# Cross-attention and block-scaled FFN on one core: GpSimd's second inverse root ahead of a partition maximum, with four lists rearranged around it

## The reference

```
query, key = ctx @ Wq.T + bq, ctx @ Wk.T + bk
attention  = softmax(query @ key.T)                    # (4, 512, 512)
x = x + layernorm(x) @ attention.T                     # stage 1
n = layernorm(x)
h = silu(mx(n) @ mx(gate_w).T) * (mx(n) @ mx(up_w).T)
x = x + mx(h) @ mx(down_w).T                           # stage 2
```

## Time and profile before

| what | value |
|---|---|
| median of 3 runs | 619.66 us (618.08 to 621.9) |
| time of the profiled execution | 622.69 us |
| its span, first to last instruction | 620.9 us |
| PE busy | 599.4 us, 97% of the span |
| DVE busy | 517.3 us, 83% |
| ACT busy | 266.3 us, 43% |
| POOL busy | 43.3 us, 7% |

### The profile page before, as it was taken

The page is one execution under the profiler, slowest core; times in us unless marked ns, Lnnn a source line. Parts: engine busy times, 40 slices in busy tenths (PEclk is TensorE's granted clock), DMA queues, the critical chain, the costliest instruction groups (busy, mean ns, idle before and its releaser), DMA issues.

```text
span 620.9 us, 7042 instructions
## 1 busy us (share of the span) xinstructions
PE 599.4 (97%) x2572; PEld 270.7 (44%) x2572; DVE 517.3 (83%) x518; ACT 266.3 (43%) x341; POOL 43.3 (7%) x49
## 2 busy tenths in 40 slices
PE   8798788999999999999999999999999999999997
PEld 3244344444444444444444444444444444444443
DVE  4999789989999989889889996888199369978931
ACT  3789678274443545542424323422132133424310
POOL 0011120210000000200000000000000001000100
PEclk9999799999999999999999999999999999999999
DMA  8949989579688676655503008400440276257670
GB/s 330 367 98 211 268 264 220 126 195 222 160 164 242 138 203 144 145 103 115 122 2 69 0 1 153 85 1 0 86 84 2 28 142 128 59 119 136 118 136 35
DMA packets 146289, 81.00 MB, mean 130 GB/s; under 512 B 134096, under 2 KB 134096, under 8 KB 142672
## 3 DMA queue, kind: packets, MB, share of 16 engines
q1 hardware_dynamic: 142512, 64.30, 43.2%
q0 software_dynamic: 3744, 16.25, 12.4%
HBM read 26.02 MB, written 8.39 MB: 55 GB/s over the span
## 4 chain that ended last, share of the span: by engine, by line
PE 76%; DVE 8%; issue 7%; DMA 4%; ACT 3%; POOL 1%; DVEq 0%; ACTq 0%; POOLq 0%
PE G L703 46%; PE A L718 27%; DMA W<-hT 3%; PE A L681 2%; DMA gu_hi<-hT 1%; DVE W L1416 1%; PE G L643 1%; DVE W L1309 1%; DVE h L1297 1%; DVE scale L1403 1%; ACT hT L884 1%; PE G L668 1%; PE A L660 1%; DVE h L1292 1%; POOL gu_lo L546 0%
## 5 line engine op out<-in xcount | busy, mean ns | idle before, releaser
L703 PE MATMUL G<-gu_hi,xT 128*128 128x512 f16 x1024 | 306.2, 379 | 0.5 <-DVE h L1457 0.5
L703 PE MATMUL G<-gu_lo,xT 128*128 128x512 f16 x512 | 194.0, 379 | 0.0
L718 PE MATMUL A<-dn,hT 128*128 128x512 f16 x768 | 167.1, 379 | 0.0
L703 PEld LDWEIGHTS G<-gu_hi,xT 128*128 128x128 f16 x1024 | 100.2, 98 | 121.9 <-issue 1.4
L718 PEld LDWEIGHTS A<-dn,hT 128*128 128x128 f16 x768 | 75.1, 98 | 90.6
L978 ACT ACTIVATE silu<-G,unscale 128x512 f32<-128x512 f32 x64 | 43.8, 685 | 146.9 <-PE G L703 121.8
L703 PEld LDWEIGHTS G<-gu_lo,xT 128*128 128x128 f16 x512 | 50.1, 98 | 60.7 <-issue 0.7
L681 PE MATMUL A<-dn,h 128*128 128x512 f32 x128 | 59.3, 619 | 8.6 <-DVE dn L1341 3.7
L1457 DVE SCALAR_TENSOR_TENSOR h<-G,unscale,silu 128x512 f32<-128x512 f32 x64 | 46.6, 736 | 14.7 <-PE G L703 13.3
L1511 DVE SCALAR_TENSOR_TENSOR W<-h,W 128x2048 f16<-128x2048 f32 x15 | 34.3, 2285 | 22.4 <-DMA hT<-W 17.8
L1292 DVE SCALAR_TENSOR_TENSOR h<-mag,h 128x2048 f32<-128x2048 bf16 x18 | 41.1, 2283 | 9.8 <-ACT mag L871 9.7
(11 more groups left out here) (92 smaller groups left out, 465.2 us busy)
## 6 DMA issues: line engine op xcount, KB each, us to landing
W<-in_units SPq DMA_DIRECT2D x12, 1024.0 KB, 5.9
W<-hT POOLq DMA_DIRECT2D x11, 1024.0 KB, 6.0
h<-in_xcols SPq DMA_DIRECT2D x4, 1024.0 KB, 12.9
out_y<-y POOLq DMA_DIRECT2D x14, 256.0 KB, 5.1
h<-in_xrows SPq DMA_DIRECT2D x3, 1024.0 KB, 12.1
out_y<-h SPq DMA_DIRECT2D x3, 1024.0 KB, 8.8
gu_hi<-in_ctxT SPq DMA_DIRECT2D x4, 512.0 KB, 10.6
W<-out_y SPq DMA_DIRECT2D x2, 1024.0 KB, 6.0
```

The costliest lines, as they stand in the source:

```text
L703: last = pe.matmul(dst[:, :], xT[:, b % 2, part, k, :], w[:, c, g, j * 512:(j + 1) * 512], start=(m == 0), stop=(m == 3 * HT - 1))
L718: last = pe.matmul(bank[:, :], hT[:, r % 2, a, k, :], dn[:, w, k, :], start=(m == 0), stop=(m == 3 * IT - 1))
```

## The change

Only the order of calls changes; no instruction is added or dropped, apart from GpSimd's exchanges of code, which are placed by the order of its calls. On SP the low part of unit 1 is transposed before three plain transfers instead of after them. On GpSimd `first_norm(1)` goes in front of `units_max(1)`. On ScalarE `take_probs(0, 0)` and both `take_projection(2, ...)` go forward, `row_variances(1)` goes forward, and `unit_hi(2)` goes behind the row sums of batch 2 and the magnitude of unit 3. On VectorE `units_power(1)` and `unit_dequant(2)` go behind the divide of unit 3, the row statistics of batch 0, its variance and one `add_attended`.

```diff
--- before.py
+++ after.py
@@ -429,10 +429,10 @@
             load_unit(3)
             after_rest("u1")
             turn_unit_hi(1)
+            turn_unit_lo(1)
             load_columns(2)
             store_rows(0)
             load_unit(4)
-            turn_unit_lo(1)
             turn_unit_hi(2)
             after_rest("u2")
             load_rows(3)
@@ -587,8 +587,8 @@
             unit_rest(0)
             after_turn("u0", 1)
             unit_rest(1)
+            first_norm(1)
             units_max(1)
-            first_norm(1)
             second_norm(0)
             after_turn("u2", 0)
             unit_rest(2)
@@ -1023,19 +1023,19 @@
             take_projection(1, 1)
             unit_magnitude(0)
             divide(0, 0)
+            take_probs(0, 0)
             exponential(1, 0)
+            take_projection(2, 0)
             row_sums(1, 0)
             row_sums(1, 1)
-            take_probs(0, 0)
+            take_projection(2, 1)
             row_sums(1, 2)
             row_sums(1, 3)
             divide(0, 1)
             row_means(1)
             exponential(1, 1)
             divide(0, 2)
-            take_projection(2, 0)
             divide(0, 3)
-            take_projection(2, 1)
             unit_magnitude(1)
             unit_hi(0)
             take_projection(3, 0)
@@ -1060,6 +1060,7 @@
             exponential(2, 3)
             row_squares(1, 2)
             row_squares(1, 3)
+            row_variances(1)
             divide(2, 0)
             take_probs(1, 0)
             take_probs(1, 1)
@@ -1067,15 +1068,14 @@
             take_probs(1, 2)
             take_probs(1, 3)
             divide(2, 1)
-            row_variances(1)
             divide(2, 2)
             divide(2, 3)
-            unit_hi(2)
             row_sums(2, 0)
             row_sums(2, 1)
             row_sums(2, 2)
             row_sums(2, 3)
             unit_magnitude(3)
+            unit_hi(2)
             row_means(2)
             exponential(3, 0)
             exponential(3, 1)
@@ -1567,15 +1567,15 @@
             add_attended(0, 3)
             unit_scale(3)
             unit_pull(2)
-            units_power(1)
             row_stats(0, 0)
-            unit_dequant(2)
             unit_divide(3)
             row_stats(0, 1)
             row_stats(0, 2)
             row_stats(0, 3)
             add_attended(1, 0)
             rows_variance(0)
+            units_power(1)
+            unit_dequant(2)
             add_attended(1, 1)
             row_max(3, 0)
             row_max(3, 1)
```

## The result

| | before | after |
|---|---|---|
| median of 12 runs each, side by side on one chip | 618.48 us (617.08 to 622.77) | 622.74 us (621.48 to 623.88) |
| time of the profiled execution | 622.69 us | 621.48 us |
| its span | 620.9 us | 619.7 us |

The changed kernel is slower: 1.0041 times the time before, 95% interval 1.0021 to 1.0061 (worked out from the rounds, so not the quotient of the two medians). Forecast was a gain of 1.4. Between the two profiled executions there is a gain of 1.2, and between the medians a loss of 4.3. The profiled execution before was among the longest of its kernel (622.77 is the only longer one of the twelve), the one after is the shortest of its twelve. So the profile after is read in two steps: was the walk of the changed kernel right, and what was it compared with.

What follows compares the result with a forecast made beforehand. TensorE's unbroken stream from the first product sets the end. Of 6.5 us, 2.2 survives the exchanges, 2.1 goes to slow clock, and earlier VectorE/ScalarE work leaves 1.4: 619.66 - 1.4 = 618.3 us, range 614.9 to 622.3.

Steps and rivals of the forecast that it cites:

- the forecast beside the median is 619.66 - 1.4: Whole kernel: the profiled execution's predicted saving of 1.4 taken off the median of the runs, giving 618.3 us.
- 6.5 us on the table: TensorE's batch 1 attends: removing a 3.74 hole and 2.77 of slow clock would end them at 76.0, not 82.5.
- `first_norm(1)` near 57.3, batch 1 in one piece to 76: GpSimd runs `first_norm(1)` before the maximum; TensorE's four batch 1 attends then run without the 3.74 hole.
- Exchange toward the maximum 6.02, away from it 9.3: GpSimd's code exchanges around the maximum: 6.02 before, 9.3 after (ends 8.4 and 10.3), with the maximum itself 2.22.
- `take_probs(2, 0)` at 80.8, attends of batch 2 at 84.2, clock falls, 2.1 charged: ScalarE gains 2.2 ahead of batch 2; TensorE's hole of some 3.5 brings the clock down, costing 2.1.
- ScalarE's early edits and the fall near 33 us hidden: Early `take_probs(0, 0)` and `take_projection(2, ...)` priced at nothing; a clock fall near 33 us hidden behind VectorE's pace.
- SP's move priced at nothing: SP's reordered transposes and loads: `unit_rest(2)` at about 77.2 against 76.8, batch 3's rows load near 82.75, no cost.
- The spread of the runs, 618.08 to 621.9, taken as noise: Earlier runs' spread: about 1% (6.2 us) is what can be told from no change; within 1% given 0.88.
- A: GpSimd's exchanges cost 6.0 both ways, `second_norm(0)` at 72.6; gain allowed 4.4, time 615.3; chance 0.16.
- B: TensorE's clock holds ahead of batch 2, the 2.1 not paid; gain 2.2 to 2.8, 616.9 to 617.5; chance 0.16.
- C: Both GpSimd exchanges take 10.26, `second_norm(0)` at 81.1; 3.7 slower, 623.4; chance 0.13.
- D: Kernel's end: the gain returns as a longer TensorE wait on VectorE's hidden product; 619.7; chance 0.12.

Runs made afterwards that it cites:

- long course: Executions of the kernel before as first profiled: maximum 2.22, exchange behind it 10.26, `first_norm(1)` at 70.66, first product at 115.64; profiled execution 622.69 us.
- short course: Executions of the unchanged kernel before with maximum 0.38, exchange behind it 8.44, `first_norm(1)` at 67.55, first product at 111.19; profiled execution 617.6 us.
- after_again: The changed kernel, unchanged, run again beside the kernel before: 623.48 us against 617.94, ratio 1.0072.
- after_noroot: The changed kernel with all inverse roots taken off GpSimd, VectorE multiplying by a constant instead: 620.43 us, ratio 1.0003.
- before_noroot: The kernel before with all inverse roots taken off GpSimd, VectorE multiplying by a constant instead: 617.69 us, ratio 0.9957.
- after_fill2: The changed kernel with 21 idle matmuls between the transposes of batch 2's probabilities, 76 to 84 us: 621.16 us, ratio 1.0000.
- after_act_back: The changed kernel with `take_probs(0, 0)` and both `take_projection(2, ...)` back in their old places on ScalarE: 623.49 us, ratio 1.0071.
- after_fill12: The changed kernel with 21 idle matmuls at 76 to 84 us and 16 more in TensorE's hole at 31.5 to 35 us: 621.74 us, ratio 1.0015.
- after_sp_back: The changed kernel with only SP's order put back, unit 1's low part behind the three plain transfers: 622.91 us, ratio 1.0052.
- after_pool_back: The changed kernel with GpSimd's old order, maximum ahead of `first_norm(1)`: 620.51 us, ratio 1.0028.
- after_loads_late: The changed kernel with the three plain transfers issued behind unit 2's high part on SP: 626.68 us, ratio 1.0104.
- before_again: The kernel before, unchanged, run again for its spread: 620.86 us (617.14 to 623.11), ratio 0.9994.
- before_fill46: The kernel before with 12 idle matmuls in TensorE's hole between batch 0's second and third attend, 46.3 to 49.3 us: 622.02 us, ratio 1.0026.
- both_front: A separate version with both inverse roots ahead of the maximum, unit 2's chain and SP's transfers moved to match: 629.77 us, ratio 1.0160.
- before_sp: The kernel before with only SP's move, unit 1's low part transposed ahead of the three plain transfers: 620.99 us, ratio 1.0035.

## Why the prediction was wrong

**The step that failed** is the last one of the sum: "the forecast beside the median is 619.66 - 1.4", 618.3, where 622.74 was measured. It took the profiled execution for an ordinary one that happens to be 3.03 long throughout, so that a saving found in it could be taken off the median. But the 3.03 were not spread over the kernel. They came with the very hole and slow clock that the change removes: the first product is 4.45 later in the long profile than in the short one. The "6.5 us on the table" lie there in the long course alone. An execution of the short course has none of it, and can only pay what the change pushes back.

That step is 3.03 of the 4.4 by which the forecast was missed. The other 1.4 is the walk itself: it gave 621.3 for the changed kernel, and the median is 622.74. The term that was too small there is the exchange away from the maximum with the power and the product behind it, 9.3 + 1.3 = 10.6: 11.72 in the profile of the shortest execution (74.39 + 2.44 less 65.11), 13.13 in after_again, the longest. In the first of these the maximum, 1.85 shorter than charged, made good for it. That the walk meets this profile to 0.3 at the product is in part luck.

**What it pays** can be read between the two profiles of the short course and of the changed kernel. `second_norm(0)` starts at 74.39 against 70.09, 4.3 later. `take_probs(2, 0)` starts at 80.40 against 77.30. The attends of batch 2 begin at 84.17 against 80.63, 3.5 later, and take 2.2 longer at the slow clock. Against that the changed kernel reaches batch 3 with less in the way (3.74 from the last attend of batch 2 to the first of batch 3, 4.99 in the short course), and has no idle 1.06 in front of the product. At the product 3.3 are left (114.48 against 111.19); in after_again it is 6.0 (117.16). The medians are 4.3 and 5.5 apart. By parts, in the group of after_again: 3.0 is the swap on GpSimd and 2.6 the other moves, by the ratios 2.7 and 1.7. The firmest figure for the other moves is after_noroot less before_noroot, 2.7, since neither of these kernels is split as the kernel before is. ScalarE's early moves are none of it.

Point by point, the steps of the prediction:

- *What bounds the kernel, and that the end follows the first product:* held in every profile, 504.6 to 505.8 us between the two.
- *`first_norm(1)` near 57.3, batch 1 in one piece to 76:* held (57.48, 75.86).
- *Exchange toward the maximum 6.02, away from it 9.3:* held in the first profile (6.21, 9.28). Over the others the second ranged from 9.28 to 10.57 with this order of transfers, so 9.3 was at the short end. The maximum's 2.22 was not paid, 0.37; the power and the product behind it were longer than 1.3 instead (2.44 to 76.83 in the first profile, 2.85 in after_again).
- *`take_probs(2, 0)` at 80.8, attends of batch 2 at 84.2, clock falls, 2.1 charged:* held in the first profile (80.40, 84.17, 0.50 from 82 to 88, 2.2), and after_fill2 shows that it is the clock. *End of batch 2 at 100.3, batch 3 at 103.9, product at 114.2:* held there (100.37, 104.11, 114.48), in the shortest execution; in after_again the same three are 103.03, 106.78 and 117.16.
- *ScalarE's early edits and the fall near 33 us hidden:* held, after_act_back and after_fill12.
- *SP's move priced at nothing:* half wrong. `unit_rest(2)` came at 77.29 as forecast and the load of batch 3's rows at 83.27, so against the long course it is nearly free. Against the short course it and the moves that came with it cost some 2 to 3 (1.7 to 3.0 by the pairs above). In that course `unit_rest(2)` came at 75.63 and the load of batch 3's rows at 81.55, 1.7 earlier than here; that this is what costs is argued and not shown.
- *The spread of the runs, 618.08 to 621.9, taken as noise:* that was the sign that was missed. Three runs, two of them 1.6 apart and the third 2.2 above, and a profile 0.8 above all of them.

**The rivals.** A (both exchanges 6.0) fell; directly behind the maximum the exchange in front of the power was never under 6.88. On this the Trainium skill, GPSIMD Engine Reference, section on instruction dispatch, has about 6 us for the first call of freshly loaded code: the trace agrees for the maximum of units 2 and 3 when none of the three plain transfers was issued ahead of the exchange (5.92 to 6.21) and not for the power. B (clock holds) fell. C (slower, once the two exchanges sum to more than 16.7) had the right sign for the wrong reason: with this order of calls they summed to 15.5 (first profile) to 16.6 (after_act_back). Its mechanism exists, though: with the transfers ahead of it the exchange toward the maximum took 9.15 (after_sp_back), so the 6.02 "with the DMA engines busy or not" did not hold for these transfers. D fell, since the span followed the first product. The rival that was needed, that the profiled execution had a loss which most executions don't have, was not among them.

**What stays open.** Why the maximum takes 1.5 to 2.5 or 0.4. Which course the 25 runs between the heaps follow, and where the long runs with a clock of 0.992 have more slow clock than the long profile. Why transfers issued ahead of an exchange make it longer. How the cost of the other moves divides between SP, VectorE and the later part of ScalarE's moves, which was never undone by itself: SP's move alone costs 3.0 in the kernel before (2.2 by the ratio), while undoing it in the changed kernel left the ratio at 1.0052, between the 1.0041 and 1.0072 of the changed kernel itself.

## What to carry to other kernels

Before a hole in a profile is counted as a gain, ask whether the profiled execution had it and the median run does not: when it lies well above the median, the gain may be there only for the long runs, and a second profile of the same kernel is the cheapest test. A gap of 2 to 3 us in front of the same attend brought down TensorE's clock in one execution and not in another, and a change that closes one gap by opening another can pay the same fall there: the four attends of batch 2 took 15.83 to 16.70 instead of 13.97 in the changed kernel's two profiles and in those of after_act_back, after_pool_back, after_sp_back and after_loads_late. Judge a swap in front of a shared unit by what it does in the best course of the kernel, since that one has no slack to pay with.

## What the runs showed of the hardware

- **The clock falls by chance on the same gap.** The profiled kernel before went through a gap of 3 us at 46.3 with the clock at 1.00; in before_again a gap of 2.15 ended at 48.62 and the clock was at 0.50 from 50 to 52. The Trainium skill, TensorE: Matmul & The Clock Gate, section "What's actually happening", says that the monitor's window runs free and does not reset when a kernel starts. The runs agree, in that one kernel takes both ways; the phase itself is in no profile here.
- **A fall of the clock can shorten a kernel.** The short course, 617 us, has the early fall at 1.7 us and is some 4 to 5 us shorter than the long one without it; with the fall prevented (before_fill46) eleven of twelve runs were long. That this goes through the exchange of code fits before_noroot: it has no exchange there, and its runs without a fall (clock 1.000) are its fastest.
- **GpSimd's exchange of code is longer when plain transfers were issued just ahead of it.** With the first of them issued 0.2 to 2.4 us ahead of the exchange it took 7.85 to 10.57 in front of the power (ten profiles) and 9.15 in front of the maximum (after_sp_back). both_front has two more: 10.29 in front of the power with transfers issued 3.6 and 2.6 ahead, and 7.47 in front of the maximum with the first of three 4.0 ahead. In front of the power the short ones had the first of the three transfers 2.2 us (after_pool_back, 6.88), 4.5 us (before_sp, 7.08) and 8.6 us (after_loads_late, 7.45, so behind its end; the DMA share over it was 0.00) behind their own start, or 10.2 us ahead of it (after_sp_back, 7.10). The mean DMA share does not tell them apart: 0.95 over the exchange of 6.88, 1.00 over the 9.28 of the first profile. So in one profile, after_pool_back, the transfers ran during most of an exchange without lengthening it, issued a little after it had begun.
- **A DMA transpose issued behind three plain transfers** held SP's queue for 8.30 to 10.09 (unit 1's low part, 1.8 to 1.9 when it went ahead of them), 9.51 (unit 2's high part, before_sp) or 12.45 (its low part, after_loads_late). With more time between the last of the three and the transpose it was shorter: 3.56 for unit 2's high part in the first profile of the changed kernel, 6.8 us behind them, and 3.80 for its low part in the kernel before, 6.0 us behind.
